# Setup of one kernel of eight images: weight preparation shared with ScalarE, and a new order of all pieces

## The reference

```python
x = x + L0(gn(x))   # triplet attention: three gates from max/mean over C, H or W, a 7x7 convolution each,
                    # mixed by a softmax over a 1-D convolution of the pooled channels
x = x + L1(gn(x))   # 3x3 convolution 256 -> 256, weights from circulant projections:
                    #   a = softmax(alphas); w = a[0]*weight
                    #   for i, b in enumerate((2, 4, 8, 16)): w = w + a[i+1] * cir_project(weight, b)
                    #   cir_project: mean over each wrapped diagonal of every b x b block of channels,
                    #   written back along the diagonals
x = x + L2(gn(x))   # squeeze and excitation on the wavelet mean (two small matrices, relu, sigmoid)
x = x + L3(gn(x))   # shifted-window attention, 8x8 windows, 8 heads, relative bias, mask
```

## Time and profile before

| | us |
|---|---|
| median of 3 runs | 2843.7 (2843.35 to 2851.99) |
| profiled execution | 2844.92 |
| its span | 2843.1 |
| TensorE busy in it | 2312.9 (81%) |
| VectorE busy | 2243.9 (79%) |
| ScalarE busy | 1621.7 (57%) |
| GpSimd busy | 1442.8 (51%) |

### The profile page before, as it was taken

The page is one execution under the profiler, slowest core; times in us unless marked ns, Lnnn a source line. Parts: engine busy times, 40 slices in busy tenths (PEclk is TensorE's granted clock), DMA queues, the critical chain, the costliest instruction groups (busy, mean ns, idle before and its releaser), DMA issues. The chain is left out here.

```text
span 2843.1 us, 67589 instructions
## 1 busy us (share of the span) xinstructions
PE 2312.9 (81%) x27254; PEld 1321.7 (46%) x27254; DVE 2243.9 (79%) x3739; ACT 1621.7 (57%) x4072; POOL 1442.8 (51%) x1149
## 2 busy tenths in 40 slices
PE   0357738898888988898888978898889988899887
PEld 0233325455554545454554445454554445444454
DVE  7887956888888887888788887888888887886444
ACT  0322037754875567654876467754876567755554
POOL 2414552455735574456635474456635574455344
PEclk9868868999999999999999999999899999999989
DMA  5400400114110421114110411114110421111111
GB/s 150 123 3 15 168 3 17 31 67 142 31 40 25 141 66 32 31 68 142 32 46 24 142 61 32 31 68 142 32 46 24 142 61 32 31 60 46 46 46 39
DMA packets 125431, 176.20 MB, mean 62 GB/s; under 512 B 72496, under 2 KB 114240, under 8 KB 115520
## 3 DMA queue, kind: packets, MB, share of 16 engines
q1 hardware_dynamic: 125120, 171.88, 19.2%
HBM read 98.95 MB, written 72.86 MB: 60 GB/s over the span
## 5 line engine op out<-in xcount | busy, mean ns | idle before, releaser
L2048 PE MATMUL F<-g_raw,cw_hi 128*128 128x512 f16 x2304 | 701.0, 386 | 54.6 <-DVE X L1462 23.0
L1172 ACT ACTIVATE xs<-xs,mx 128x64 f32<-128x64 f32 x1792 | 445.8, 335 | 79.4 <-DVE mx L1813 79.4
L892 POOL TENSOR_TENSOR xs<-xs,rec 128x512 f32<-128x512 f32 x256 | 292.7, 1153 | 344.5 <-DVE rec L1823 343.5
L2048 PE MATMUL F<-g_raw,cw_lo 128*128 128x512 f16 x1152 | 444.0, 385 | 0.0
L2048 PEld LDWEIGHTS F<-g_raw,cw_hi 128*128 128x128 f16 x2304 | 222.0, 99 | 327.0 <-DVE X L1462 30.3
L1179 ACT ACTIVATE prt<-PTR 128x512 f32<-128x512 f32 x256 | 151.4, 591 | 259.2 <-PE PTR L2149 229.7
L877 POOL TENSOR_TENSOR tmp<-X,uw 128x512 f32<-128x512 f32 x128 | 164.4, 1299 | 253.8 <-DVE X L1658 236.2
L907 POOL TENSOR_TENSOR ot_lo<-ot,ot_hi 128x512 f16<-128x512 f32 x128 | 153.7, 1222 | 221.2 <-ACT ot_hi L1193 182.2
L1802 DVE TENSOR_TENSOR xs<-SP,bias 128x1024 f32<-128x1024 f32 (+2 forms) x192 | 160.2, 862 | 117.0 <-issue 67.2
L1391 DVE SCALAR_TENSOR_TENSOR g_raw<-l0c,gn,g_raw 128x512 f16<-128x512 f32 x192 | 183.2, 996 | 55.6 <-ACT g_raw L1031 40.0
L1821 DVE TENSOR_REDUCE sums<-xs 128x16 f32<-128x1024 f32 x128 | 154.9, 1210 | 79.8 <-ACT xs L1167 42.3
(11 more groups left out here) (326 smaller groups left out, 5725.3 us busy)
## 6 DMA issues: line engine op xcount, KB each, us to landing
scratch_x<-X SPq DMA_DIRECT2D x32, 1024.0 KB, 4.8
xs<-scratch_x SPq DMA_DIRECT2D x56, 508.0 KB, 3.4
out_x<-xs SPq DMA_DIRECT2D x56, 508.0 KB, 2.8
X<-in_x SPq DMA_DIRECT2D x25, 1024.0 KB, 6.4
l0c<-scratch_t SPq DMA_DIRECT2D x8, 1876.0 KB, 10.2
l0c<-in_x SPq DMA_DIRECT2D x7, 1024.0 KB, 5.0
l0c<-scratch_t SPq DMA_DIRECT2D x8, 640.0 KB, 12.2
l0c<-scratch_t SPq DMA_DIRECT2D x8, 576.0 KB, 13.5
```

The lines of the kernel that those rows point to most:

```text
L892: G.tensor_tensor(keyed(sc[:, u % 4, :]), keyed(sc[:, u % 4, :]), rec[:, u % 4, :].unsqueeze(2).to_broadcast([P, 8, TOK]), ALU.mult).then_ ...
L1172: last = S.activation(keys, keys, ACT.Exp, bias=mx[:, u % 4, i:i + 1])
L2048: last = T.matmul(F[:, n % 2, :], wgt[:, ci, C3 * comp + dx, P * co:P * co + P], win[which], start=(ci == 0 and dx == 0 and j == 0), stop= ...
```

## The change

Own share goes to ScalarE. The sums of diagonals of all four block sizes come first, without a copy: the first sum reads the weights themselves, each block size has its own place in tcs. Then ScalarE writes the turned and scaled diagonals (tcrs), in two instructions a block size, over the weights in xs, and VectorE adds them. In the six rounds ScalarE writes six scaled rows instead of three (a quarter, sixths, a 24th), so that VectorE's rows need no scale afterwards; the high halves are two wide instructions instead of six, the low halves two wide tensor_tensor instead of six with a scale. The high halves of the attention weights go to ScalarE, and VectorE's low halves read the unscaled weights with the scale. FIRST, TURN, AHEAD and LAST_ROWS are new for all engines, so the whole sequence of pieces differs.

```diff
-    "SP": {"norm0b": "Y", "reduce3": "Y", "hwconv": "Y", "hwrows": "Y", "band1": "Z", "hwmean2": "F", "gate3": "Z",
-        "gate13": "G", "conv1.1": "Z", "conv2.0": "F", "conv3.1": "F", "conv8.1": "Z", "conv10.1": "F",
-        "conv21.1": "L"},
+    "SP": {"reduce2": "Y", "reduce4": "Y", "reduce8": "Y", "gate1": "Y", "gate4": "Z", "gate5": "G", "gate7": "Z",
+        "conv4.0": "F", "conv4.1": "F", "conv5.0": "Z", "conv11.1": "F", "conv12.1": "F", "conv20.1": "Z",
         "conv21.1": "L"},
...
+    "POOL": {"load": "R", "norm0a": "RRYR", "reduce0": "R", "reduce2": "RR", "reduce4": "RY", "reduce5": "R",
+        "reduce8": "RR", "reduce10": "R", "reduce13": "RRRR", "zpool": "RR", "hwgate": "R", "bandcopy": "RR",
+        "bandturn": "R", "hwmean3": "R", "hwmean4": "RR", "hwmean5": "R", "hwmean7": "R", "logits": "R",
+        "conv2.0": "D", "conv2.1": "DDD", "conv3.0": "DY", "conv4.0": "D", "conv6.1": "W", "conv8.0": "W",
...
+    "DVE": {"load": "CUCYCUCYCCCCUCCUYYYUYYCCCCYCC", "norm0b": "Y", "norm0c": "Y", "reduce1": "YYYYY",
+        "reduce3": "Y", "reduce4": "YY", "reduce5": "U", "reduce6": "U", "reduce9": "U", "reduce11": "Y",
+        "reduce12": "UU", "reduce13": "U", "reduce14": "U", "reduce15": "UUUYU", "hwrows": "YY", "band1": "Y",
+        "band2": "Y", "logits": "YY", "mixturn": "Y", "gate1": "Y", "gate2": "Y", "gate14": "Y", "norm1b": "Y",
...
-    "SP": {"reduce2": "S", "reduce4": "LS", "reduce12": "L", "band2": "SL", "bandturn": "S", "hwmean4": "L",
-        "gate6": "SL", "gate13": "Z", "gate14": "S", "conv1.1": "L", "conv2.0": "F", "conv3.1": "Z", "conv8.0": "S",
-        "conv9.1": "F", "conv13.1": "LG", "conv14.1": "F", "conv17.0": "Z", "conv18.0": "S", "conv21.1": "F",
-        "conv23.0": "ZL"},
+    "SP": {"norm0b": "LS", "norm0c": "G", "reduce3": "L", "reduce4": "S", "reduce11": "L", "band2": "SL",
+        "bandturn": "S", "hwmean3": "LS", "hwmean7": "L", "logits": "S", "gate1": "L", "gate2": "ZF", "gate3": "S",
+        "gate4": "Z", "gate11": "L", "gate16": "F", "conv7.0": "F", "conv7.1": "Z", "conv12.1": "S",
+        "conv14.0": "Z", "conv19.1": "F"},
...
+                    act.wait_ge(setup_shares, 1)
+                    act.wait_ge(wconv_in, 16 * (P // BMAX))
+                    S.activation(acc, WB, ACT.Copy, scale=al[:, 1, 0:1]).then_inc(setup_own, 1)
+                    yield "own share"
+                    act.wait_ge(setup_tc, 1)
+                    act.wait_ge(setup_own, 1)
+                    for n, b in enumerate(BLOCKS):
+                        src, dst = (ap.rearrange("p (q k c) -> p q k c", k=b, c=TAPS) for ap in (tcs[n], tcrs[n]))
+                        S.activation(dst[:, :, 0, :], src[:, :, 0, :], ACT.Copy, scale=shares[:, n:n + 1])
+                        S.activation(dst[:, :, 1:b, :], src[:, :, b - 1:0:-1, :], ACT.Copy,
+                                     scale=shares[:, n:n + 1]).then_inc(setup_tcr, 1)
+                        yield "turned round"
...
-                        for i in range(C3):
-                            last = S.activation(wu[i], setup_banks(n)[:, i, :], ACT.Copy, scale=gm[:, 4:5])
+                        for to, g, scale in ((6, g0, g_sixth), (7, g2, g_sixth), (3, g0, g_24th), (4, g1, g_sixth),
+                                             (0, g0, g_quarter), (5, g2, gm[:, 4:5])):
+                            last = S.activation(wu[to], g, ACT.Copy, scale=scale)
...
-                        for comp, (row, scale) in enumerate(KERNEL_ROWS):
-                            S.activation(cw_hi[:, ti, C3 * comp + dx, :], wu[row], ACT.Copy, scale=scale
-                                         ).then_inc(setup_hi, 1)
+                        for high, rows in kernel_parts(n, cw_hi):
+                            S.activation(high, rows, ACT.Copy).then_inc(setup_hi, 1)
...
+                    act.wait_ge(setup_q, 1)
+                    for t in range(CT):
+                        S.activation(qkv_hi[:, t, :], qkv_f[t], ACT.Copy, scale=gm[:, 5:6]).then_inc(setup_q_hi, 1)
+                    S.activation(wo_hi[:, :, :], wo, ACT.Copy, scale=wm[:, 2:3]).then_inc(setup_q_hi, 1)
...
+                def diagonals(n, b):
+
                     for j in range(1, b):
-                        V.tensor_tensor(diag(tc, b, 0, b - j), diag(tc, b, 0, b - j), blocks(WB, b, j, j, b - j), ALU.add)
-                        seq.link(V.tensor_tensor(diag(tc, b, b - j, j), diag(tc, b, b - j, j), blocks(WB, b, j, 0, j),
-                                                 ALU.add))
+                        for lo, count, at_ in ((0, b - j, j), (b - j, j, 0)):
+                            so_far = blocks(WB, b, 0, lo, count) if j == 1 else diag(tcs[n], b, lo, count)
+                            last = V.tensor_tensor(diag(tcs[n], b, lo, count), so_far, blocks(WB, b, j, at_, count), ALU.add)
...
-                    for i in range(b):
-                        last = V.tensor_scalar(diag(tcr, b, i, 1), diag(tc, b, (-i) % b, 1), al[:, 1, n + 1:n + 2],
-                                               1.0 / b, ALU.mult, ALU.mult)
-                    seq.link(last)
-                    yield "turned round"
+                def circulant(n, b):
+
+                    dve.wait_ge(setup_tcr, n + 1)
...
+                        for i, ((low, rows), (high, _)) in enumerate(zip(kernel_parts(n, cw_lo), kernel_parts(n, cw_hi))):
+                            dve.wait_ge(setup_hi, 2 * n + i + 1)
+                            V.tensor_tensor(low, rows, high, ALU.subtract).then_inc(setup_lo, 1)
...
-                    for t in range(CT):
-                        seq.link(V.tensor_scalar(qkv_f[t], qkv_f[t], gm[:, 5:6], None, ALU.mult))
-                        seq.link(V.tensor_copy(qkv_hi[:, t, :], qkv_f[t]))
-                        V.tensor_tensor(qkv_lo[:, t, :], qkv_f[t], qkv_hi[:, t, :], ALU.subtract)
-                        yield "halves"
...
+                    for t in range(CT):
+                        dve.wait_ge(setup_q_hi, t + 1)
+                        V.scalar_tensor_tensor(qkv_lo[:, t, :], qkv_f[t], gm[:, 5:6], qkv_hi[:, t, :], ALU.mult, ALU.subtract)
+                    yield "halves"
```

More of the change, by code:

```diff
@@ L302, in build, with kernel_parts @@
         wu_sets = [[q[:, i, :] for q in quarters[2 * s:2 * s + 2] for i in range(4)] for s in range(2)]
+        def kernel_parts(n, cw):
+            ti, dx = divmod(n, C3)
+            first, second = quarters[2 * (n % 2):2 * (n % 2) + 2]
+            return ((cw[:, ti, dx:dx + 3 * C3 + 1:C3, :], first[:, 0:4, :]),
+                    (cw[:, ti, dx + 4 * C3:dx + 5 * C3 + 1:C3, :], second[:, 0:2, :]))
         consts_in = sem("consts_in")
@@ L423, in build @@
         setup_perm = sem("setup_perm")
+        setup_shares = sem("setup_shares")
+        setup_own = sem("setup_own")
+        setup_tc = sem("setup_tc")
+        setup_tcr = sem("setup_tcr")
+        setup_q = sem("setup_q")
+        setup_q_hi = sem("setup_q_hi")
         pads_zero = sem("pads_zero")
@@ L448, in build @@
         tc_both = cw_lo[:, :, :, :].rearrange("p t k c -> p (t k c)").bitcast(fp32)
-        tc = tc_both[:, 0:BMAX * BMAX * TAPS]
-        tcr = tc_both[:, BMAX * BMAX * TAPS:2 * BMAX * BMAX * TAPS]
+        level_at = [sum(BMAX * 2 * BMAX // b * TAPS for b in BLOCKS[:n]) for n in range(len(BLOCKS) + 1)]
+        tcs = [tc_both[:, lo:hi] for lo, hi in zip(level_at, level_at[1:])]
+        tcrs = [xs[:, lo:hi] for lo, hi in zip(level_at, level_at[1:])]
+        shares = al[:, 0, 0:len(BLOCKS)]
+        g_quarter, g_sixth, g_24th = (al[:, 1, i:i + 1] for i in range(3))
         qkv_f = [prt[:, :, :].rearrange("p a n -> p (a n)")[:, 0:3 * C], ot[:, :, :].rearrange("p a n -> p (a n)")[:, 0:3 * C]]
@@ L988, in setup @@
                         if n >= 2:
-                            act.wait_ge(setup_lo, COMPS * (n - 1))
-                        for i in range(C3):
-                            last = S.activation(wu[i], setup_banks(n)[:, i, :], ACT.Copy, scale=gm[:, 4:5])
+                            act.wait_ge(setup_lo, 2 * (n - 1))
+                        g0, g1, g2 = (setup_banks(n)[:, i, :] for i in range(C3))
+                        for to, g, scale in ((6, g0, g_sixth), (7, g2, g_sixth), (3, g0, g_24th), (4, g1, g_sixth),
+                                             (0, g0, g_quarter), (5, g2, gm[:, 4:5])):
+                            last = S.activation(wu[to], g, ACT.Copy, scale=scale)
                         last.then_inc(setup_g, 1)
@@ L1239, in diag @@
                     return v[:, :, :, lo * TAPS:(lo + count) * TAPS]
[L1241 to L1244 removed]
+                def diagonals(n, b):
                     for j in range(1, b):
[L1246 to L1248 removed]
+                        for lo, count, at_ in ((0, b - j, j), (b - j, j, 0)):
+                            so_far = blocks(WB, b, 0, lo, count) if j == 1 else diag(tcs[n], b, lo, count)
+                            last = V.tensor_tensor(diag(tcs[n], b, lo, count), so_far, blocks(WB, b, j, at_, count), ALU.add)
```

(42 more changed lines are left out.)

41 lines of the change are left out of this document (19 added, 22 removed), and 122 rows, old and new, of tables (FIRST, TURN).

## The result

The changed kernel takes **2805.0 us** (median of 4 runs, 2798.6 to 2807.1), the kernel before beside it 2846.0: a ratio of **0.9846, 95% interval 0.9831 to 0.9861**. It is faster by 41 us, more than three times the 12 us forecast, and lies outside the range given. The profiled execution took 2804.5 us (span 2802.7) against 2844.9 (span 2843.1), so 40.4 us are to be explained.

The account below looks back on a forecast made before the run. In image 0 VectorE's kernel additions, GpSimd's late maximum and VectorE's convolution work bound in turn. Gains of 8.8 and 4.4, orders 0, made 13.2 off 2844.9: 2831.7, say 2832 us; forecast 2825 to 2840, eight in ten 2817 to 2856.

Parts of the forecast that it names:

- Setup up to the first convolution: Image 0's start: kernel finished 2.3 us earlier, first convolution 8.8 us earlier, at 213 or 214.
- So the 9.2 goes: Image 0's convolutions: VectorE's 9.2 us stand for GpSimd's maxima vanishes, as they move to conv2 and conv3.
- The stand for the fetch: Image 0's convolutions: image 1's fetch queues behind the constants, so VectorE stands 10 us at image 1's first maximum; ends 0, 15.
- The sum for image 0: First convolution 8.8 us earlier plus 4.4 in the convolutions: image 1 starts 13.2 us earlier.
- The saved 5.2 of VectorE's work: Image 0's convolutions: scaling and rounding of qkv (4.3) and output weights (0.9) leave VectorE, 5.2 us gained.
- The new orders ... I take 0, and allow 1.5 an image, 10 in all: Later images: tables hold the same pieces, so reordering gains 0; allowance 1.5 us an image, 10 in all.
- Rival 4: Later images: the orders alone win 1.5 us an image, 2821 us; chance 0.16 together with rival 1 (no fetch stand, 2822).
- The condition for "wrong": Images 2 to 6: periods leaving 319.5 us by over 1.5 would mean the orders decide, not the setup.
- Rival 3: TURN: gate3's row store behind first store and fetch starves TensorE; at 4 us an image, 2860 us; chance 0.16.
- The price of a copy: Setup up to the finished kernel: the copies leaving VectorE were counted as 2.9 us.

Follow-up runs that it names:

- version 9: Changed kernel with attention-weight maxima early, image 1's fetches ahead of the constants, and a one-column GpSimd addition behind the maxima: 2778.4 us, 0.9760 of the kernel before.
- 12: Kernel before (old setup, old image 0 order) with new TURN, AHEAD, LAST_ROWS, early maxima and the small GpSimd addition: 2789.7 us, 0.9798 of the kernel before.
- versions 1: Changed kernel with the old TURN, AHEAD and LAST_ROWS, so new setup and image 0 order only: 2852.1 us, 1.0030 of the kernel before.
- 2: Kernel before with the new TURN, AHEAD and LAST_ROWS, so old setup and old image 0 order: 2796.8 us, 0.9833 of the kernel before.
- version 6: Changed kernel with attention-weight maxima early and, in image 0, image 1's fetches ahead of the constants: 2787.5 us, 0.9790 of the kernel before.

## Why the prediction was wrong

- **Setup up to the first convolution: right.** Kernel finished at 93.2 (93), the wait for the turned level 2.6 (2.5), Z at 136.5 (136), first convolution at 214.4 (213 to 214).
- **"So the 9.2 goes": wrong.** It stayed, as 9.0, at conv8 as before. The step took it that maxima placed at conv3 are over when VectorE comes to conv8. GpSimd was late itself and in them from 246.7 to 261.5, VectorE came at 256.6, and the addition it needed stood behind them until 265.1. Moving both engines' maxima to 141 took the stand away; that the gap is some 7 us into plain additions, paid later if they come later, was hidden in the earlier trace rows as the idle before 108.84 and 272.45, which I read as the length of the maxima.
- **The stand for the fetch: right in its mechanism**, the fetch behind the constants behind the last low half, and its removal gave 8 to 11. That the size fits, 9.2 for 10, is luck in part: the quarter landed 17.9 after the low half (15 forecast), and VectorE came for it 8.7 after (5 forecast); the two errors cancel.
- **The sum for image 0: wrong by 16.5**, 3.3 later instead of 13.2 earlier (by 13.3 to 15.6 in the other versions with this image 0). 9.0 are the kept stand, 0.9 the first convolution. The saved 5.2 of VectorE's work hardly reached the path: freed of stands, the convolutions take 105.7 with the new code and 106.7 with the old, and VectorE is busy for 94.8 of them against 95.6. The moved work left, but other small setup operations took longer (in version 9 against 12, two bias additions 1.9 us for 0.8, one scaling of two numbers 1.16 for 0.16). The remainder, about 1.5, is in other waits of that stage, 3.7 at 244.8 the longest, and in scatter; no run splits it.
- **"The new orders ... I take 0, and allow 1.5 an image, 10 in all": the step that failed.** They were worth 3.7 in each of images 2 to 6 and 20.9 at the end, together with images 1 and 7 some 44 us in the profiled executions and 47 by the medians of versions 1 and 2. I compared the tables by counts of pieces for each stage, and the last rows not at all; TensorE's idle there, 48 of 216 us at a clock of 0.90, would have shown that this stretch had much to give: it is 22% of its time, against 12% in an ordinary image. Rival 4 had the sign and, for the images, the place, with 2.2 us an image too little and nothing for the end. The condition for "wrong" that I had set, periods off 319.5 by over 1.5, is the one that came.
- Rival 3 (the row store behind the fetch) did not come: no period grew.
- The price of a copy that I cited from the Trainium skill ("VectorE: DVE Perf Modes") could not be tested at 768 numbers: in the kernel before and in versions 2 and 12, each of these copies ran beside additions on GpSimd and took 1.50 to 1.51 us. The copy of 512 numbers, with GpSimd idle, took 0.43 in all three. Nothing of the result hangs on it.

What stays open: which letters within TURN save the 3 us in the convolutions, and which of LAST_ROWS the 21 at the end. The waits that went are named above, but the tables of TURN were only exchanged together, or GpSimd's alone, and that one run mixes effects.

## What to carry to other kernels

When all queues' orders are laid out anew, forecast each stretch by its idle time and its clock, the drain at the end first, and don't price an order at nothing because its counts are equal. An order of one engine can't be judged by putting it back alone: the one mixed set tried in the images lost 22 us an image against the old set and 25 against the new. And a gain in a start-up stage is only worth what no later stand takes back: here the rewritten setup was worth nothing (0.1 to 0.3% slower) until the fetch and the maxima had been moved, and 7 us then.

## What the runs showed of the hardware

- After an all-partition maximum, GpSimd's next TENSOR_TENSOR starts 6.6 to 7.6 us late, with no instruction in that time, in all 28 cases of the 14 traces (among them 105.65, 261.51, 151.66, 198.95), even when copies and memsets run in between without delay. A maximum straight behind additions started 5.8 to 6.2 us after the last of them, with nothing to wait for (10 cases); where GpSimd already stood waiting for VectorE's reduce, it started 0.1 to 0.2 us after that (144.17 in version 6, 98.40 after the change).
- VectorE operations of 256 numbers with both inputs in SBUF that take 0.42 us alone took 2.29 to 2.55 us beside GpSimd's additions on 1024.
- The same 2818 matmuls: 171.0, 169.1, 165.2, 162.6 and 156.8 us busy at granted clocks of 0.87, 0.89, 0.93, 0.93 and 0.96, with 53.8, 49.7, 55.2, 48.7 and 37.9 us idle. The busy time follows the clock within some 3%; the clock does not follow the idle time.
